# One more part of the scores drained ahead of the exponentials

## The reference, cut to what matters

```python
dots = jnp.einsum('bhid,bhjd->bhij', q, k) * SCALE
dots = jnp.einsum('bhij,hk->bkij', dots, pre_proj)
dots = jnp.where(causal, NEG_INF, dots)
topk_vals = jax.lax.top_k(dots, K)[0]          # K = 64
dots = jnp.where(dots < topk_vals[..., -1:], NEG_INF, dots)
attn = jax.nn.softmax(dots, axis=-1)
out = jnp.einsum('bhij,bhjd->bhid', attn, v)
```

## Time and profile before

| | |
|---|---|
| median of 3 runs | 2712.11 us (2709.88 to 2712.58) |
| profiled execution, own time | 2717.66 us |
| its span, first to last instruction | 2715.9 us |
| PE, DVE, ACT, POOL busy | 81%, 81%, 58%, 21% of the span |
| the loop over the 64 groups | from about 334 us to about 2470 us |
| granted TensorE clock, mean | 0.907 of full |

### The profile page before, as it was taken

The page is one execution under the profiler, slowest core; times in us unless marked ns, Lnnn a source line. Parts: engine busy times, 40 slices in busy tenths (PEclk is TensorE's granted clock), DMA queues, the critical chain, the costliest instruction groups (busy, mean ns, idle before and its releaser), DMA issues. The chain is left out here.

```text
span 2715.9 us, 34880 instructions
## 1 busy us (share of the span) xinstructions
PE 2206.3 (81%) x10182; PEld 1299.0 (48%) x10182; DVE 2204.6 (81%) x9006; ACT 1574.5 (58%) x2342; POOL 570.0 (21%) x427
## 2 busy tenths in 40 slices
PE   6599646677777758888888989899895799988997
PEld 3566434334444424444454445555553455545665
DVE  1512599999999989899999888998998999998445
ACT  1121234455666636767777777777774788875222
POOL 0000002222223213222222233223231131422000
PEclk9599666789889979999999999999998899989999
DMA  2000000000000000000000000000000000002000
GB/s 66 1 0 0 16 1 1 1 1 1 1 1 1 1 0 1 1 1 1 1 1 1 1 1 1 1 1 1 1 1 1 1 1 1 1 3 69 1 1 16
DMA packets 18068, 13.64 MB, mean 5 GB/s; under 512 B 6972, under 2 KB 15814, under 8 KB 17862
## 3 DMA queue, kind: packets, MB, share of 16 engines
q1 hardware_dynamic: 13824, 8.92, 1.2%
q10 hardware_dynamic: 4038, 2.37, 0.3%
HBM read 9.19 MB, written 2.10 MB: 4 GB/s over the span
## 5 line engine op out<-in xcount | busy, mean ns | idle before, releaser
L903 PE MATMUL bank<-hT,qT 128*128 128x512 f32 (+3 forms) x1280 | 581.7, 591 | 205.8 <-ACT R L580 120.6
L1238 DVE MAX8 cand<-R 128x8 f32<-128x12 f32 (+15 forms) x4096 | 685.8, 220 | 5.7 <-ACT R L580 3.7
L935 PE MATMUL bank<-WP,Y 128*128 128x512 f32 x1088 | 588.7, 635 | 0.5 <-ACT WP L637 0.2
L447 POOL TENSOR_TENSOR X<-R,X 128x144 f32<-128x144 f32 (+15 forms) x64 | 168.2, 2628 | 1875.7 <-ACT X L623 1875.7
L919 PE MATMUL bank<-ident,R 128*128 128x128 f32 x2176 | 440.8, 286 | 49.3 <-ACT WP L637 34.7
L903 PEld LDWEIGHTS bank<-hT,qT 128*128 128x128 f32 x1280 | 240.7, 207 | 468.2 <-issue 192.3
L630 ACT ACTIVATE R<-R,negm 128x144 f32<-128x144 f32 (+15 forms) x256 | 309.7, 1212 | 181.6 <-DVE F L1309 181.6
L920 PE MATMUL bank<-nidentb,F 128*128 128x128 bf16 x2176 | 407.4, 223 | 0.0
L919 PEld LDWEIGHTS bank<-ident,R 128*128 128x128 f32 x2176 | 313.8, 144 | 194.6 <-issue 80.9
L637 ACT ACTIVATE WP<-bank 128x512 f32<-128x512 f32 x544 | 317.9, 593 | 95.8 <-PE bank L920 84.6
L580 ACT ACTIVATE R<-bank 128x1024 f32<-128x1024 f32 (+7 forms) x384 | 290.9, 772 | 127.9 <-PE bank L903 70.2
(11 more groups left out here) (243 smaller groups left out, 2714.7 us busy)
## 6 DMA issues: line engine op xcount, KB each, us to landing
R<-in_L_attn_Wkv ACTq DMA_DIRECT2D x2, 512.0 KB, 7.9
out<-X SPq DMA_DIRECT2D x1, 1024.0 KB, 5.1
R<-in_L_ffn_gate_w SPq DMA_DIRECT2D x1, 1024.0 KB, 7.0
R<-in_L_ffn_up_w SPq DMA_DIRECT2D x1, 1024.0 KB, 9.6
out<-X SPq DMA_DIRECT2D x4, 256.0 KB, 2.3
R<-in_L_attn_Wq ACTq DMA_DIRECT2D x1, 512.0 KB, 6.2
WP<-in_L_attn_Wo ACTq DMA_DIRECT2D x1, 512.0 KB, 11.0
R<-in_L_ffn_wi SPq DMA_DIRECT2D x1, 256.0 KB
```

Source lines behind the costliest of these rows:

```text
L447: pool.tensor_tensor(OV[i - 2][:, 0:n], S[:, k % NS, i, 0:n], OV[i - 2][:, 0:n], ALU.subtract)\
L903: last = pe.matmul(to, qT[:, k % 2, i, :], hT[:, a:b], start=True, stop=b < n, skip_group_check=True)
L935: pe.matmul(bank[6], Y[:, j, :], PT[:, (blocks_before(k) + j) % 4, :], start=(j == 0), stop=(j == k // 4))\
L1238: mark(dve.max(cand[:, :, c, i], lists(S[:, k % NS, i, 0:n], n, c)))
```

## The change

One number in `late_from` goes from 1 to 2. The early part of each group then has one slot more, the first of unit 2. In groups 0 to 31 this is all of unit 2: ScalarE drains m, s0, s1, s2 in front of the exponentials of the group before, and only q and s3 between them. In groups 32 to 63 it is the first of unit 2's two slots; the second, q, and the two of unit 3 stay late. No instruction is added or removed, and the lists of TensorE, VectorE and GpSimd are the same.

```diff
             def late_from(k):
 
-                return 1 + 2 * slots(k // 4)
+                return 2 + 2 * slots(k // 4)
 
             def drain_early(k):
                 for name in slots_of(k)[:late_from(k)]:
```

## The result

The changed kernel takes 2745.35 us (median of four runs, 2743.5 to 2749.2) against 2712.35 before: ratio 1.0125, 95% interval 1.0108 to 1.0143. That is 33 us slower; the forecast was 11 us, with a range that ended at 2735. The profiled span is 2742.1 us against 2715.9.

The account below looks back on a forecast made before the run. Each period was taken as VectorE's own work plus its wait for ScalarE's last count. Full-clock sum -3.8 and clock term +14.8 gave +11 us on 2712.1, so 2723 us; range 2705 to 2735.

Parts of the forecast that it names:

- Rivals 1 and 2: 1: clock stays up at the cut, 2708 us, chance 0.34; 2: VectorE's last-count wait shrinks, 2701 us, chance 0.10.
- The full-clock sum, -3.8 us: Without clock effects, VectorE's wait on the last count shrinks in some groups, plus 0.5 at the end: -3.8 us.
- The clock term, +14.8 us: Behind lengthened full-bank waits at the cut, TensorE's blocks run at half clock and VectorE waits: +14.8 us.
- seven of ten waits ahead of the scores: Before the change, TensorE ran at 1.2 GHz behind 7 of 10 waits of 3.1 to 4.7 us.
- The two durations that made up the 1.4: Extra time of one cold block on TensorE: 0.60 us for its transposes and 0.81 for its product.
- Rival 3: Groups 53 to 62: pushed exponentials reach the cut, up to 0.9 us a period, 2720 us or 2731 with clock; chance 0.10.
- the bounds of +8 and -6: Limits in us on the change's effect in groups 53 to 62, where a gain of 0.5 us was taken.
- the push of 1.8: Groups 53 to 62: first exponential delayed 1.8 us by a fill wait and one drain, given back before the heads drain.

Follow-up runs that it names:

- the fill experiment: The changed kernel plus nine unused matmuls at TensorE's wait with both banks full, only in groups 20 to 51: 2710.56 us, 0.9985.
- the first experiment: The changed kernel, with TensorE made to wait ahead of the outputs for the third exponential of the group: 2743.55 us, 1.0118.
- the high-groups kernel: The changed kernel, with the moved slot only from group 32 on: 2741.37 us, 1.0098.
- the last experiment: The changed kernel, with ScalarE draining four turned blocks ahead of the cut instead of three in periods 20 to 57: 2686.65 us, 0.9903.
- the best: The changed kernel, with five turned blocks drained ahead of the cut in periods 20 to 52 and four in 53 to 57: 2683.44 us, 0.9893.

## Why the prediction was right and wrong

**The mechanism was right.** The forecast said that TensorE's idling would move to the cut, that the clock would fall behind it and that VectorE would wait; all three stand in the rows above, and the fill experiment shows that the clock is the cause. Rivals 1 and 2 fall, since VectorE's wait is 130.1 us and not 97 or less. The size was a third of what came, and the range, which ended at 2735, missed.

**The full-clock sum, -3.8 us.** The kernel filled in groups 20 to 51, called the fill kernel from here on, shows it nearly alone. Its groups 20 to 31 sum to 377.1 us, the kernel before has 380.9: -3.8, where the forecast had -3.3 for them. Group 26 came from 3.14 to 1.63 us of wait, as forecast; group 28 to 1.21 in the fill kernel, and to 2.67 in the changed one, where it is cold. The fill kernel's whole loop is 2118.0, only 1.3 under before, since group 56 was not filled and cost 1.7, and the last groups lost a little. Without group 56 it is -3.0. Of both differences 0.9 is the clock's: groups 21 and 22 were cold before and are filled here. Without these two it is -2.9 for groups 20 to 31 and -2.1 for the loop, so the term was right to within 2 us.

**The clock term, +14.8 us: this step failed.** The fill kernel's periods, taken from those of the changed kernel, give it stretch by stretch, from the timelines (both have the same order, so what they differ by is the clock and the filling):

| groups | forecast: cold, us | measured: cold, us |
|---|---|---|
| 20 to 24 | two more, 0.8 | two more, 1.4 with the two that were cold before |
| 25 to 31 | 5 of 7, 7.0 | 3 of 7, 4.1 |
| 32 to 35 | 2 of 4, 2.8 | 3 of 4, 6.2 |
| 36 to 47 | 3 of 12, 4.2 | 9 of 12, 16.7 |
| 48 to 52 | none | 2 of 5, 3.1 |

The sum, 31.5 (of it 1.0 for the two groups that were cold before too), is nearly the whole loss. Up to group 35 the term came out close, 10.6 us against 11.7, but by luck: too many cold groups in 25 to 31 and too few in 32 to 35 offset each other. From group 36 on it failed, 4.2 us against 19.8. Three things made the whole twice the term. First, and most of it, the number of cold groups in groups 32 to 52: 14 of 21, where 5 of 16 were counted and the last five left out; at the forecast's own 1.4 us the 14 are 19.6 us and not 7.0. Their waits were longer than worked out. For groups 36 to 47 the forecast took 1.3 us onto what it saw before and came to 2.0 to 2.5; they are 1.67 to 3.60, 2.90 in the mean, eight of them over 3.0. ScalarE's wait for the cut in these twelve groups went from 1.91 in the mean to 4.34, by 2.4 and not 1.3 us. The clock itself fits the missing 1.1 us: before, q and the scores ran in part at 1.2 GHz, which had shortened the lead; with their wait gone they run at full clock, so the lead grows by what they gain as well. In the twelve periods that end with the cuts of groups 36 to 47 the score matmuls (L903) take 184.3 us before and 171.1 after, 1.1 a period. No run isolates this. The forecast named those cold spells ahead of the cut and called them free, but it took the lead from the rows that held them.

The share of cold ones among such waits was too low as well. The forecast took five of seven and two of four for waits of 3 us and more, and 14 of 15 came. The count behind it, seven of ten waits ahead of the scores, looked too near to the wait: behind two of the three that it took as fast, the clock fell a little later, as here in the kernel before, 1.2 us later at 653.48, where four matmuls take 2.39 us and not 1.32:

```profile
652.27 1.32 PE L903 MATMUL bank<-hT,qT 128*128 128x512 f32 x4 [3.97 <-ACT R L576]
...
653.48 2.39 PE L903 MATMUL bank<-hT,qT 128*128 128x512 f32 x4
```

With these two it is nine of ten; the ten include the two waits that the forecast named as its ends.

Second, the price of a cold block is 1.65 us and not 1.4. In group 33 the period went from 33.58 to 35.23, VectorE's wait from 2.59 to 4.25. The two durations that made up the 1.4 leave out what a block costs until the next can start: in group 34 the transposes start at 1240.44 and at 1243.58, 3.14 us apart, where full speed gives a block in 1.59, so that a cold one costs 1.55 there.

Third, groups 34, 43 and 44 had two cold blocks each, at 2.9 us in group 34, and the forecast knew only one. VectorE's wait in group 43, against 3.14 before:

```profile
1590.38 0.16 DVE L1355 SCALAR_TENSOR_TENSOR tie<-r,cutb 128x4 f32<-128x4 f32 x1 [6.15 <-ACT signs L607]
```

In the other direction it was too high in groups 25 to 31: only groups 25, 28 and 30 were cold (group 30 behind 2.11 us), since groups 26, 27, 29 and 31 had waits of 1.5 to 2.3 us and not of 3.8.

**Rival 3**, the pushed exponentials of groups 53 to 62. Without group 56 these nine periods sum to 433.1 us against 431.8, +1.3, within the bounds of +8 and -6. Groups 61 (44.78 to 46.41) and 62 lost 2.6, groups 57 and 58 gained 1.2. Nothing is seen of 0.9 a period. The forecast also said that it would be wrong if these exponentials came over 0.3 us a period later. They did, by 1.4 to 2.0 us in most of these periods, about the push of 1.8 that it had worked out itself; but the drain of the heads behind them came 0.9 us later at most where the period was not cold. So the sign was badly chosen, and the push was given back, as the forecast said. Group 56 is no push: its 1.7 us are the clock, behind a wait of 3.04.

**The signs that were named.** L630's wait for the mask was to fall by some 40 us and fell by 82. The waits of L903 and L885 on L580 were to fall to less than half: together they went from 209.4 to 89.3 us, but L903's alone only to 81.0. L623's wait for the cut was to grow by 40 to 60 and grew by 119, 44 of it in groups 0 to 20, which I had not counted and where it costs nothing. The wait with full banks was to grow by 40 to 60 and grew by 76. The wait on the last count was to be 110 or more and is 130.1. Each sign pointed the right way, and the waits at the cut grew by more than said, in the later groups because the lead was worked out too small.

**The rule that spoke against it.** The Trainium skill's "TensorE: Matmul & The Clock Gate", section "HAM oscillation — how this bites in real kernels", lets every burst behind a long idle gap start cold. The forecast had applied it to all of groups 21 to 35, whose waits it put at 3.0 us and more, and came to 17 us for them; measured are 11.7. The trace of the changed kernel agrees for the longer waits, 14 of 15 from 3.0 us on. In groups 21 to 35 ten of 15 were cold, and for the shorter waits it is about half (counts below).

## What to carry to other kernels

An engine with a clock that falls when it idles has no free wait: ask of every wait that a change lengthens not only who waits for that engine now, but which work comes right behind it, at half speed. Work out a lead that a change makes from durations at full clock, since the cold spell that the change removes was part of the old lead. When an edit gives an engine a lead, spend it in the same edit (here up to two more blocks ahead of the cut: 33 us slower became 29 us faster), and judge by where the clock is low, not by its mean.

## What was not expected

How often a wait was followed by 1.2 GHz, over all waits with full banks of groups 20 to 61 in the changed kernel: 3.0 us and more, 14 of 15; 2.6 to 3.0, four of seven; 2.0 to 2.6, four of eight; under 2.0 or no wait at all, none of twelve. The length of the wait alone doesn't decide: 2.89 us in group 32 stayed fast, 2.89 in group 34 cost two blocks. Group 45 waited 3.32 us in the changed kernel and stayed fast, and 3.31 us in the kernel of the first experiment and in the high-groups kernel, where it was cold. The 1.92 us of group 40 in the last experiment, and 1.95 us of group 31 in the first, show that under 2.0 it can happen too. The clearest pair is group 25, in the kernel before and in the one that changes the high groups only, which has the same order up to there. TensorE's wait and VectorE's wait on the last count, before:

```profile
931.53 0.33 PE L919 MATMUL bank<-ident,R 128*128 128x128 f32 x1 [2.55 <-ACT WP L637]
...
939.32 0.16 DVE L1355 SCALAR_TENSOR_TENSOR tie<-r,cutb 128x4 f32<-128x4 f32 x1 [1.61 <-ACT signs L607]
```

and in the high-groups kernel:

```profile
929.44 0.33 PE L919 MATMUL bank<-ident,R 128*128 128x128 f32 x1 [2.55 <-ACT WP L637]
...
938.10 0.16 DVE L1355 SCALAR_TENSOR_TENSOR tie<-r,cutb 128x4 f32<-128x4 f32 x1 [2.48 <-ACT signs L607]
```

The same wait of 2.55 us, and only in the second did the clock fall behind it. So it is not settled by the order of the program and the length of the wait, and from these rows the cold groups can only be forecast as a share. What decides stays open.

The mean granted clock ranks the kernels badly: 0.907 for before and changed, 33 us apart; 0.929 for the fill kernel at 2710.56; 0.913 for the best at 2683.44.

The part ahead of the loop took between 339 and 351 us in executions of kernels that are the same there, so a difference of some us between two spans says nothing until the loop is taken by itself: the spans of before and after differ by 26.2, the loops by 30.4, the medians by 33.
